# Layer norm statistics in one operation per tile, square roots on ScalarE, and routing with tokens on partitions

## What is computed

```python
x = x + attn_a(layernorm(x))     # x: 2 x 1024 tokens x 128
x = x + ffn(layernorm(x))
x = x + attn_b(layernorm(x))
x = x + ffn(layernorm(x))        # the same weights again

def layernorm(x): return (x - mean(x)) / sqrt(var(x) + 1e-5)

def attn_a(x):    # causal differential attention over 1024 tokens, 16 heads
    ...
    out = out * rsqrt(mean(out * out) + EPS) * gamma   # per head of 8 values
    return (0.8 * out) @ w_proj

def ffn(x):
    base = x @ W.T
    proj = l2norm(x @ Wp.T + bp)                 # 32 values per token
    lw = softmax(proj @ l2norm(sim) * exp(min(temp, CLAMP_MAX)))  # 4 experts
    ret = where(arange(4) == argmax(lw), lw, 0)
    return base + sum_e ret[e] * (x @ Wd[e].T) @ Wu[e].T   # ranks 1, 2, 4, 8

def attn_b(x):    # per token: softmax attention of 64 x 64 in each of 16 heads
    ...
```

## Time and profile before

| | |
|---|---|
| Median of 3 runs | 2138.11 us (2136.70 to 2138.21) |
| Profiled execution | 2138.5 us, of which the span from the first to the last instruction is 2136.7 us |
| a1 with its barrier | 0 to 53.3 us |
| a2 | 53.3 to 587 us |
| a3 | 588 to 607 us |
| f1 | 607.6 to 660.3 us |
| b, head up to the first product of a chunk | 660.9 to 703.7 us |
| b, the 16 tiles | 703.7 to 2079 us |
| f2 | 2079.5 to 2134.0 us, then the last store |

### The profile page before, as it was taken

One profiled execution on the slowest core, in us unless ns is written; L12 is line 12 of the kernel. 1 busy time (PEld: TensorE's weight loads), 2 busy tenths in 40 slices (PEclk: granted clock), 3 DMA queues, 4 the chain that ended last, 5 costly groups with the idle time before them and its releaser, 6 DMA issues. The chain is left out here.

```text
span 2136.7 us, 35583 instructions
## 1 busy us (share of the span) xinstructions
PE 1847.3 (86%) x14162; PEld 1368.3 (64%) x14226; DVE 1884.3 (88%) x1607; ACT 1108.5 (52%) x1448; POOL 1414.5 (66%) x661
## 2 busy tenths in 40 slices
PE   2799999999756699898998998988989989889877
PEld 1344444444244578777787787777877877778776
DVE  6978887887254899999999999999999999999973
ACT  2267776776611355554545555545455555454540
POOL 5122222222201789889899898898998988989961
PEclk9899999999965899999999999999999999999996
DMA  3300000000000000000000000000000000000000
GB/s 100 64 5 8 8 6 8 9 5 2 1 0 0 1 1 1 2 1 2 1 1 2 1 1 2 1 1 2 1 1 2 1 1 1 2 1 1 1 1 20
DMA packets 10981, 14.46 MB, mean 7 GB/s; under 512 B 4656, under 2 KB 7632, under 8 KB 10672
## 3 DMA queue, kind: packets, MB, share of 16 engines
q1 hardware_dynamic: 9264, 11.31, 2.2%
q10 hardware_dynamic: 1536, 0.63, 0.1%
HBM read 4.57 MB, written 1.05 MB: 3 GB/s over the span
## 5 line engine op out<-in xcount | busy, mean ns | idle before, releaser
L1057 POOL TENSOR_TENSOR b_p_ring<-b_p_ring,b_m 128x2048 f32<-128x2048 f32 (+7 forms) x384 | 1250.9, 3299 | 139.9 <-DVE b_p_ring L969 137.9
L1095 ACT ACTIVATE b_p_ring<-b_p_ring 128x2048 f32<-128x2048 f32 (+7 forms) x384 | 532.7, 1412 | 640.8 <-POOL b_p_ring L1057 640.8
L1158 PE MATMUL b_ps<-k_ident,b_ev_ring 128*128 128x128 f32 (+6 forms) x4608 | 579.7, 276 | 121.7 <-DVE b_ev_ring L1015 121.5
L1015 DVE TENSOR_TENSOR b_ev_ring<-b_p_ring,b_ps 128x2048 f32<-128x2048 f32 (+7 forms) x384 | 634.1, 1655 | 1.7 <-ACT b_p_ring L1095 1.7
L969 DVE TENSOR_TENSOR b_p_ring<-b_ps,b_key 128x2048 f32<-128x2048 f32 (+7 forms) x384 | 634.4, 1660 | 0.0
L1158 PEld LDWEIGHTS b_ps<-k_ident,b_ev_ring 128*128 128x128 f32 (+6 forms) x4608 | 491.3, 135 | 183.3 <-DVE b_ev_ring L1015 159.1
L1158 PE MATMUL b_ps<-k_ident,b_p_ring 128*128 128x128 f32 (+6 forms) x4608 | 567.9, 273 | 19.5 <-ACT b_p_ring L1095 12.5
L1158 PEld LDWEIGHTS b_ps<-k_ident,b_p_ring 128*128 128x128 f32 (+6 forms) x4608 | 504.7, 135 | 26.1 <-ACT b_p_ring L1095 12.8
L564 DVE TENSOR_REDUCE a_negm<-a_ps 128x1 f32<-128x768 f32 (+7 forms) x384 | 354.5, 954 | 89.4 <-PE a_ps L453 88.1
L547 ACT ACTIVATE a_ex<-a_ps 128x512 f32<-128x512 f32 (+3 forms) x768 | 334.3, 497 | 189.3 <-PE a_ps L492 174.9
L384 POOL TENSOR_SCALAR_AFFINE_SELECT a_ex<-a_ex 128x512 f32<-128x512 f32 x128 | 81.6, 638 | 364.4 <-ACT a_ex L547 363.9
(11 more groups left out here) (163 smaller groups left out, 1065.6 us busy)
## 6 DMA issues: line engine op xcount, KB each, us to landing
rk_of_group<-rows_k SPq DMA_DIRECT2D x96, 32.0 KB, 2.0
rq<-rows_q SPq DMA_DIRECT2D x42, 64.0 KB, 2.3
k_wqkv<-in_wqkv SPq DMA_DIRECT2D x1, 2048.0 KB, 8.4
out<-x_all SPq DMA_DIRECT2D x4, 256.0 KB, 2.4
k_wo<-in_wo SPq DMA_DIRECT2D x1, 512.0 KB, 9.2
rq<-rows_q SPq DMA_DIRECT2D x12, 32.0 KB, 1.9
k_w_attn<-in_w_attn ACTq DMA_DIRECT2D x1, 192.0 KB, 2.8
k_reset_max<-in_reset_max ACTq DMA_DIRECT2D x1, 128.0 KB, 4.9
```

What stands on the lines that cost most here:

```text
L1015: nc.vector.tensor_tensor(chunk(ev_ring, c), chunk(p_ring, c), over_queries(values(c), c), ALU.mult).then_inc(ev_done.sem, 1)
L1057: nc.gpsimd.tensor_tensor(pc, pc, over_rows(m[:, half].rearrange("p i h -> p (i h)"), c), ALU.subtract).then_inc(shifted.sem, 1)
L1095: nc.scalar.activation(pc, pc, ACT.Exp).then_inc(exp_done.sem, 1)
L1158: last = nc.tensor.matmul(ps[0:width, bank, b // IB * P:(b // IB + 1) * P], rows[:, r, b:hi].rearrange("p i h -> p (i h)"), k["ident"][:], ...
```

## The change

The layer norm: one `bn_stats` per tile on DVE gives, for the even and for the odd elements of a token, the mean and the sum of squared deviations. Five operations on 128x16 elements join them into the variance and the mean (a sixth, the sum of the means, runs beside the root), ACT takes the square root, and DVE the reciprocal. Each piece is then normalised in two operations (subtract the mean, multiply) where there was one. POOL has no part in it any more. ACT runs a one-column square root before it waits, so that the table of functions is loaded then.

Routing: one product per tile with `wroute` (the down projections and the router's projection side by side, 64 columns) replaces L825, L827, L831 and L832. Bias, squares, sum of squares and the four dot products (`dots`, 128x2048) are DVE operations with tokens on partitions; the root is ACT's. The small operations that follow are 12 instead of 14, since the maximum is found before the exponential.

The head of b: `keys_by_head` comes first and each half has a PSUM bank of its own, so have the keys; nothing on PE waits between. The scans come before the addition of `bo` to x on DVE.

In a1 the norm of `sim` is two DVE operations, not a product of PE, and its root ACT's. Loads: `wroute` replaces two tensors, and `sim`, `temp` and `bp` come as rows for all partitions. With one load fewer in the list, which SP and ACT share alternately, the 2 MB of `wqkv` are issued by ACT as its sixth transfer instead of by SP as its sixth. In a2, POOL multiplies `w_proj` (128x128) by gamma, and the four multiplications by gamma in a3 (L658) are gone.

```diff
-            layernorm_statistics(nc, dve, stat_step, x_all[:], xn, sq, st, 0)
-            dve.wait_ge(rstd_ready.sem, 1)
-            for s in range(S):
-                nc.vector.tensor_tensor(xn[:, piece(s)], xn[:, piece(s)],
-                                        st[:, 3, piece(s)].unsqueeze(2).broadcast_to([P, FT, D]), ALU.mult).then_inc(xn_ready.sem, 1)
+            layernorm_statistics(nc, dve, stat_step, rstd_ready, x_all, xn, bn, st)
+            for s in range(S):
+                normalize(nc, dve, xn_ready, s, x_all, xn, st, piece(s))
...
                 parts(nc.vector, dve, q_step, rows_q, 0, s)
 
-            dve.wait_ge(norm_ready.sem, 1)
+            dve.wait_ge(exps_done.sem, 3)
...
-            pool.wait_ge(stat_step.sem, 5)
-            nc.gpsimd.tensor_tensor(st[:, 3, :], st[:, 2, :], k["pw"][:, 0:TILES], ALU.pow).then_inc(rstd_ready.sem, 1)
-            pool.wait_ge(const_step.sem, 5)
-            nc.gpsimd.tensor_tensor(t32[:, 2, :], t32[:, 1, :], k["ph"][0:PROJ, 0:E], ALU.pow).then_inc(norm_ready.sem, 1)
...
+            root_of_variance(nc, act, stat_step, rstd_ready, st, k["ph"])
 
             def copy_xnT(s):
                 act.wait_ge(xnT_psum.sem, s + 1)
...
             turn(0)
-            pe.wait_ge(filled.sem, 3)
-            pe.wait_ge(const_step.sem, 4)
...
-    dve.wait_ge(step.sem, step.next(it))
-    nc.vector.tensor_reduce(st[:, 1, :], sq[:], X, ALU.add).then_inc(step.sem, 1)
-    dve.wait_ge(step.sem, step.next(it))
-    nc.vector.tensor_scalar(st[:, 2, :], st[:, 1, :], 1.0 / D, EPS, ALU.mult, ALU.add).then_inc(step.sem, 1)
+    for t in range(n):
+        last = nc.vector.bn_stats(bn[:, t, :], x[:, t, :])
+    last.then_inc(step.sem, 1)
+    dve.wait_ge(step.sem, step.next(0))
+    even, odd = bn[:, :, 0:3], bn[:, :, 3:6]
+    nc.vector.tensor_tensor(row(0), even[:, :, 1], odd[:, :, 1], ALU.subtract).then_inc(step.sem, 1)
+    nc.vector.tensor_tensor(row(1), even[:, :, 2], odd[:, :, 2], ALU.add).then_inc(step.sem, 1)
+    step.next(0)
+    dve.wait_ge(step.sem, step.next(0))
+    nc.vector.tensor_tensor(row(2), row(0), row(0), ALU.mult).then_inc(step.sem, 1)
+    nc.vector.tensor_scalar(row(1), row(1), 1.0 / D, EPS, ALU.mult, ALU.add).then_inc(step.sem, 1)
+    step.next(0)
+    dve.wait_ge(step.sem, step.next(0))
+    nc.vector.scalar_tensor_tensor(row(3), row(2), half * half / D / D, row(1), ALU.mult, ALU.add).then_inc(step.sem, 1)
+    step.next(0)
+    nc.vector.tensor_tensor(row(0), even[:, :, 1], odd[:, :, 1], ALU.add).then_inc(step.sem, 1)
+    dve.wait_ge(step.sem, step.next(0))
+    dve.wait_ge(root_ready.sem, 1)
+    nc.vector.reciprocal(row(3), row(2)).then_inc(step.sem, 1)
+    dve.wait_ge(step.sem, step.next(0))
+    step.check()
+
+
+def normalize(nc, dve, step, s, x, xn, st, piece):
+
+    m = st[:, 0, piece].unsqueeze(2).broadcast_to([P, FT, D])
+    r = st[:, 3, piece].unsqueeze(2).broadcast_to([P, FT, D])
+    nc.vector.scalar_tensor_tensor(xn[:, piece], m, -0.5, x[:, piece], ALU.mult, ALU.add).then_inc(step.sem, 1)
+    dve.wait_ge(step.sem, 2 * s + 1)
+    nc.vector.tensor_tensor(xn[:, piece], xn[:, piece], r, ALU.mult).then_inc(step.sem, 1)
+
+
+def root_of_variance(nc, act, step, root_ready, st, warm):
+
+    nc.scalar.activation(warm[:, 1:2], warm[:, 0:1], ACT.Sqrt)
+    act.wait_ge(step.sem, ROOT_STEP)
+    nc.scalar.activation(st[:, 2, :], st[:, 3, :], ACT.Sqrt).then_inc(root_ready.sem, 1)
 
 
...
             nc.gpsimd.memset(mrows[:], 0.0).then_inc(ready.sem, 1)
...
             for s in range(S):
                 dve.wait_ge(o_psum.sem, s + 1)
...
+            nc.scalar.activation(ms[:, 3, 0:1], ident[:, 0:1], ACT.Sqrt)
...
-            for s in range(S):
-                dve.wait_ge(p_psum.sem, s + 1)
-                nc.vector.tensor_scalar(pr[:, 0, cols(s)], ps_b[0:PROJ, cols(s)], k["bp"][:], None, ALU.add).then_inc(pr_ready.sem, 1)
-                dve.wait_ge(pr_ready.sem, 2 * s + 1)
-                nc.vector.tensor_tensor(pr[:, 1, cols(s)], pr[:, 0, cols(s)], pr[:, 0, cols(s)], ALU.mult).then_inc(pr_ready.sem, 1)
-            dve.wait_ge(l_psum.sem, 1)
-            nc.vector.tensor_copy(lg[:, :, 0:E + 1], ps_l[:, :, 0:E + 1]).then_inc(route_step.sem, 1)
+            layernorm_statistics(nc, dve, stat_step, rstd_ready, x_all, xn, bn, st)
+            for s in range(S):
+                normalize(nc, dve, xn_ready, s, x_all, xn, st, piece(s))
+
+            for half in range(2):
+                tiles = slice(half * TILES // 2, (half + 1) * TILES // 2)
+                dve.wait_ge(r_psum.sem, half + 1)
+                nc.vector.tensor_tensor(pr[:, 0, tiles], ps_r[:, tiles, DOWN:DOWN + PROJ],
+                                        k["bp"][:].unsqueeze(1).broadcast_to([P, TILES // 2, PROJ]), ALU.add).then_inc(pr_ready.sem, 1)
+            dve.wait_ge(pr_ready.sem, 2)
+            nc.vector.tensor_tensor(pr[:, 1], pr[:, 0], pr[:, 0], ALU.mult).then_inc(route_step.sem, 1)
             dve.wait_ge(route_step.sem, route_step.next(0))
+            nc.vector.tensor_reduce(row(0), pr[:, 1], X, ALU.add).then_inc(route_step.sem, 1)
+            route_step.next(0)
+            nc.vector.tensor_tensor(dots[:], pr[:, 0].unsqueeze(2).broadcast_to([P, TILES, E, PROJ]),
+                                    k["simn"][:].unsqueeze(1).broadcast_to([P, TILES, E, PROJ]), ALU.mult).then_inc(route_step.sem, 1)
+            dve.wait_ge(route_step.sem, route_step.next(0))
+            nc.vector.tensor_reduce(g[:, 1], dots[:], X, ALU.add).then_inc(route_step.sem, 1)
...
-            nc.vector.tensor_scalar(row(0), row(7), 1e-12, None, ALU.max).then_inc(route_step.sem, 1)
+            route_step.next(0)
+            nc.vector.tensor_scalar(row(2), row(1), 1e-12, None, ALU.max).then_inc(route_step.sem, 1)
             dve.wait_ge(route_step.sem, route_step.next(0))
-            nc.vector.reciprocal(row(1), row(0)).then_inc(route_step.sem, 1)
+            nc.vector.reciprocal(row(3), row(2)).then_inc(route_step.sem, 1)
             dve.wait_ge(route_step.sem, route_step.next(0))
-            nc.vector.tensor_tensor(g[:, 0], lg[:, :, 0:E], bc(1), ALU.mult).then_inc(route_step.sem, 1)
+            nc.vector.tensor_tensor(g[:, 0], g[:, 1], bc(3), ALU.mult).then_inc(route_step.sem, 1)
             dve.wait_ge(route_step.sem, route_step.next(0))
...
+            nc.vector.scalar_tensor_tensor(g[:, 3], g[:, 1], 0.0, k["rank4"][:].unsqueeze(1).broadcast_to([P, TILES, E]),
+                                           ALU.is_ge, ALU.mult).then_inc(route_step.sem, 1)
...
+            dve.wait_ge(exp_done.sem, 1)
+            nc.vector.tensor_reduce(row(6), g[:, 2], X, ALU.add).then_inc(route_step.sem, 1)
...
+            nc.vector.tensor_tensor(g[:, 5], g[:, 4], g[:, 2], ALU.mult).then_inc(route_step.sem, 1)
+            route_step.next(0)
+            nc.vector.reciprocal(row(7), row(6)).then_inc(route_step.sem, 1)
             dve.wait_ge(route_step.sem, route_step.next(0))
-            nc.vector.tensor_reduce(row(6), g[:, 5], X, ALU.max).then_inc(route_step.sem, 1)
...
+            nc.vector.tensor_tensor(g[:, 0], g[:, 5], bc(7), ALU.mult).then_inc(chosen.sem, 1)
...
-        def _(pool):
-            pool.wait_ge(stat_step.sem, 5)
-            nc.gpsimd.tensor_tensor(st[:, 3, :], st[:, 2, :], k["pw"][:, 0:TILES], ALU.pow).then_inc(rstd_ready.sem, 1)
-            pool.wait_ge(route_step.sem, 1)
-            nc.gpsimd.tensor_tensor(r1[:, 7, :], lg[:, :, E], k["ph"][:, 0:TILES], ALU.pow).then_inc(norm_ready.sem, 1)
-
...
+            act.wait_ge(route_step.sem, 2)
+            nc.scalar.activation(r1[:, 1, :], r1[:, 0, :], ACT.Sqrt).then_inc(norm_ready.sem, 1)
+            nc.scalar.activation(k["ph"][:, 1:2], k["ph"][:, 0:1], ACT.Exp)
...
-            for s in range(S):
-                pe.wait_ge(xnT_ready.sem, s + 1)
-                nc.tensor.matmul(ps_b[0:PROJ, cols(s)], k["wpT"][:], xnT[:, cols(s)], start=True, stop=True).then_inc(p_psum.sem, 1)
-            for n in range(TILES):
-                nc.tensor.matmul(ps_d[:, n, :], xnT[:, tile(n)], k["wdT"][:], start=True, stop=True)
-            for n in range(TILES):
-                if n % FT == 0:
-                    pe.wait_ge(pr_ready.sem, 2 * (n // FT) + 2)
-                nc.tensor.matmul(ps_l[:, n, 0:E], pr[:, 0, tile(n)], k["simn"][:], start=True, stop=True)
-                last = nc.tensor.matmul(ps_l[:, n, E:E + 1], pr[:, 1, tile(n)], k["ones32"][:, 0:1], start=True, stop=True)
-            last.then_inc(l_psum.sem, 1)
+            for half in range(2):
+                pe.wait_ge(xnT_ready.sem, 2 * half + 2)
+                for n in range(half * TILES // 2, (half + 1) * TILES // 2):
+                    last = nc.tensor.matmul(ps_r[:, n, :], xnT[:, tile(n)], k["wroute"][:], start=True, stop=True)
+                last.then_inc(r_psum.sem, 1)
...
-            pe.wait_ge(chosen.sem, 1)
+            pe.wait_ge(chosen.sem, 2)
...
```

(18 more changed lines are left out.)

175 lines of the change are left out of this document (73 added, 102 removed).

## The result

| | before | after |
|---|---|---|
| Median, beside each other on one chip | 2137.40 us (4 runs) | 2083.55 us (4 runs, 2082.35 to 2085.98) |
| Ratio | | 0.9754, 95% interval 0.9737 to 0.9771 |
| Span of the profiled execution | 2136.7 us | 2082.5 us |

The account below looks back on a forecast made before the run. DVE (88% busy) and PE (86%) mostly fill the unchanged loops; savings come from serial stretches between. a1 8.2, a3 1.6, f1 18.5, b 15.4, f2 20.2: 63.9 us off 2138.5 gives 2074.6 us, range 2064 to 2088 us.

Parts of the forecast that it names:

- rival (1): PE's clock stays at half in routing products, tails and b's head: 10.3 us more, 2085 us; chance 0.14.
- PE's clock never rises in the routing: Sign in the feed-forwards' routing that would show the prediction to be wrong; no size given.
- Layer norm statistics: Layer norm: 16 operations at 0.20 us, 3.3 us in all; first piece after 4.7 us, not 12.47; 7.8 us saved.
- Rival (2): Dear statistics: 2080 us at the lone operation's price, 2086 us at the scan's price; chance 0.12.
- Normalising: Layer norm in f1, b and f2: two operations per piece with a wait between, for one; 2.2 us lost.
- Routing products: PE in f1 and f2: 16 products of 64 columns at 0.28 us, 4.5 us; ends 3.8 and 6.9 us.
- DVE's part: Routing in f1 and f2: DVE takes 9.3 us from the last routing product to the weighting.
- Tails: End of each feed-forward from the turning of the weighted projections: 2.0 us lost in f1, 0.3 us in f2.
- Head of b: First tile's copy to maxima 14.8 us instead of 23.1, plus 1.5 us for a clock rise; 9.8 us saved.
- a1: First stretch: the second turn starts at 17.15, not 25.70; 8.2 us saved.
- Rival (3): Six more ACT table loads on the path, 1.28 us each, 7.7 us together, 2082 us; chance 0.03.
- Rival (4): Slower than before: new ring buffer addresses slow b's 768 large DVE products, 2151 us at 0.1 us each; chance 0.01.

Follow-up runs that it names:

- e7: The changed kernel with each piece normalised tile by tile, one DVE operation with both scalars per tile instead of two operations per piece; 2064.35 us, ratio 0.9664.
- e9: The changed kernel with PE waiting in f1 and f2 for the fourth normalised piece before it turns the first; 2077.07 us, ratio 0.9733.
- e11: The changed kernel with one more 128-column product, result overwritten, after the four turns of each piece in f1 and f2; 2073.14 us, ratio 0.9695.
- e1: The changed kernel with four unread filler products on PE before the tail, ahead of the wait for the chosen ranks, in f1 and f2; 2072.61 us, ratio 0.9701.
- e2: The changed kernel with four filler products at the start of PE's part of f1 and f2; 2081.02 us, ratio 0.9741.
- e6: The changed kernel with the old order at the head of b: queries first, keys by head after the keys' taking; 2091.94 us, ratio 0.9792.
- e4: The changed kernel with the old routing: separate narrow products, POOL's power, and the norm of `sim` by a product in a1; 2100.39 us, ratio 0.9829.
- e3: The changed kernel with four filler products both at the front and before the tail of f1 and f2; 2072.43 us, ratio 0.9703.
- e5: The changed kernel with the old layer norm in all four places: four passes, POOL's power, one operation per piece; 2099.61 us, ratio 0.9822.
- e8: The changed kernel with tile-by-tile normalising and four filler products both at the front and before the tail of f1 and f2; 2061.34 us, ratio 0.9645.
- e10: The changed kernel with tile-by-tile normalising and seven filler products before the tail, none at the front; 2063.34 us, ratio 0.9649.

## Why the prediction was right, and what was mis-sized

The mechanisms on DVE and at the head of b were right, and the time fell into the range since the range had been drawn to hold rival (1) alone. The point forecast was 10 us too hopeful for one reason, PE's clock in the feed-forwards (2.4 and 3.0 us in each); 1.9 us more than forecast in a1 and a3 made up for a little of it. One of the prediction's own signs of being wrong, that PE's clock never rises in the routing, came true for the routing products: all 16 ran at 0.50 in f1 and in f2. The loops stayed: a2 took 535.3 us and b's tiles 1375.7 us. A table load before a root whose wait had been released does occur, for the norm of `sim` in a1 (32.69 us, 1.28 us long), but it cost nothing: SP's transfers end a1, at 42.88 us. Before the roots of the three layer norms and two routings in f1, b and f2 there is none.

- **Layer norm statistics: right.** 0.20 us each in a row, 3.19 us for 16 (forecast 3.3), first piece after 4.66 us (4.7). Rival (2), dear statistics, is out. The Trainium skill ("VectorE: DVE Perf Modes", section on the TRN2 errata) advises tiles of 512 elements or more, since each small one pays a fixed latency. At the 0.29 us of a lone operation the 16 would have taken 4.6 us; the row shows 0.20 us each, so it does not speak against this operation in a row.
- **Normalising: the 2.2 us were right, their consequence was not seen.** The head of b from its first statistic to the first tile's copy went from 17.86 to 12.18 us, 5.7 us against 5.6. What two operations per piece do to PE's pace was no step of the working, and what PE's pauses do to its clock stood only in rival (1); e7, e9 and e11 show it, and it is behind the routing products' part of the loss.
- **Routing products: mis-sized.** 4.5 us assumed, "since f1's clock rose after about as much PE work"; 6.93 us measured, the upper end that was named. Before, that work was 16 turns without a pause and then products of 512 columns; now the turns have pauses, and products of 64 columns follow. 2.4 us in each. The rows before gave a warning that was not read: f2's clock rose about 6 us after its first turn (2092.72), where f1's took about 3 (620.87).

```profile
624.00:625.00 1.00, 1.00 (x5) 0.89 0.00 0
...
2098.00:2100.00 2.00, 2.00 (x5) 0.80 0.00 0
```

- **DVE's part: right.** 9.2 us from the end of the routing products (614.50) to the weighting (623.69); 9.3 forecast.
- **Tails: mis-sized.** 6.4 + 2.0 and 8.2 + 0.3 us, so about 8.4 each, taken from f2's pace before; 11.4 measured, the clock at half to the end. 3.0 us in each. e1 shows it to be the clock alone. Part of this is chance: f2 of e2 and of e6, with the same work and 5.1 us of idle time before it, took the 8.4 us that were forecast.
- **Head of b: mechanism right, 1 us high.** 14.3 us to the maxima, where the forecast was 14.8 less 1.5. Without any rise it would have been 14.8: of the 2.2 us that a rise was held to be worth, 0.5 came, since it came late. When it comes is not fixed: behind the same layer norm the same head took 14.7 us in e2 and e11, 13.3 in e9, 13.1 in e1 and 12.0 in e4.
- **a1: 1.6 us low.** The second turn started at 17.15 to the hundredth. From there to the first spreading it took 10.5 us and not 11.8 as before: the first four products with `w_attn` behind this turn took 2.58 us, not 3.62. Their pace shows a clock that rose sooner (the windows of a1 list 1.00 throughout and do not show it). This was luck: with the same a1, e1, e2, e6 and e11 took 11.8 us again, and e3 and e9 10.4.
- **Rival (1)** was thus the right one for f1 and f2 (2 x 5.4 us) and not for b's head; a1 and a3 gave 2 us back, hence 2083.6 and not 2085. **Rival (3)**: the trace has seven more loads, not six; the one at 616.67 is 1.28 us and covered, and no block is longer than forecast for one. The Trainium skill's 2.66 us per switch ("ScalarE: Activation LUTs", What ACT_TABLE_LOAD costs) is not seen: the load follows the root's end (616.66) at once. **Rival (4)** is out, b's tiles took 1375.7 us.

The chance of 0.14 for rival (1) was too low for what its own rows said. The stretch at 0.50 in the earlier trace rows is not one of "little PE work": PE is busy for 4.00 of its 4.00 us, with products of one to four columns. So products without a pause, if narrow, can run at half for long, and the argument against the rival ("then 11 us of dense products follow") needed a clock that rises in time for the first 7 of them.

## What to carry to other kernels

Price a PE stage at both clocks, and ask what the change does to the pauses in the PE work ahead of it: an operation more per piece on the engine that feeds PE cost here more by the clock (3.2 us in the routing products) than by its own time (1.6 us), and beside e5's f1 a layer norm that was 5.6 us quicker gave nothing. Where a chain hands PE small pieces, try a quicker hand-over (1.03 us per piece did here what 1.33 us did not), or fill the pauses with a product whose result is thrown away; four small ones per feed-forward were worth 6.9 us in the two, apart from the tail. Look at f1 and f2 both, and at more than one kernel with the same stretch, before a difference of 1 to 3 us is put down to an edit. A step that stands in another engine's queue (the norm of `sim`) should be looked for again when the work around it gets quicker.

## What the runs showed of the hardware

- Of 10 feed-forwards in which PE turned a piece and then waited for the next, 1.33 us apart (after, e1, e2, e3, e6), none had a full clock in the routing products, not even where it was full at the first turn. Of 12 whose pieces came 1.03 us apart or closer, or with a product between (e5, e7, e8, e9, e10, e11), 10 had it (3.68 to 4.44 us) and two had not (6.93 us, e5 and e10, both in f2). What tells these two apart isn't settled. In the twelve at half clock it rose only behind the routing products, in the products with W.
- After an idle time of 4 to 6.3 us ahead of the turning, the tail's turns and products took either 10.7 us (half clock to the end, 6 of 14 cases) or 7.7 us (a rise some 3 to 4 us in), from the same program: e5 has 7.7 in f1 and 10.7 in f2, e11 the reverse. With 0 to 2.3 us idle (e1, e3, e4, e10) they took 5.7 to 5.9 us in all eight cases, with 2.9 us (e8) 7.7 and 6.4. The kernel before is the exception: after 1.56 us idle f1 took 5.7 us, after 1.93 us f2 took 7.4 us. What sets it apart isn't settled. Executions of one kernel may differ by such an either-or, as e9's times suggest.
- Stretches of the same code differ from kernel to kernel: in after, e1, e2, e3, e6, e9 and e11 SP's first spreading starts between 27.50 and 28.98 us, a3 takes 16.2 to 17.7 us, and b's tiles 1374.0 to 1375.9 us.
- A DVE operation over 128x128 f32 with two scalars from memory takes 0.26 us in a row, the statistics operation 0.20 us.
